# A long convolution on TensorE: sixteen chunks written out, or a loop of two chunks over fixed places

## What is computed

```python
dt = exp(log_dt); A = -exp(A_log)                       # 256 channels, 64 states
K = einsum('mn,mln->ml', C_re, exp(dt * A * t))         # one kernel of 512 taps for each channel
y = irfft(rfft(u, 2L) * rfft(K, 2L))[:L]                # causal convolution, channel by channel
x1 = x + y + u * D
```

## Time and profile before

| | |
|---|---|
| runs (us) | 989.84, 991.02, 986.16 |
| profiled execution, its own time (us) | 987.75 |
| its span, first to last instruction (us) | 985.9 |
| mean granted TensorE clock | 0.972 |
| busy share of the span | PE 93%, PEld 79%, ACT 53%, DVE 42%, POOL 29% |
| recurrence, about | 12 to 378.5 us of the span |
| convolution, first weight load of line 568 to the last addition's end | 388.3 to 463.0 us |
| chain that ended last | PE 85%, issue 5%, DVE 4%, ACT 4% |

### The profile page before, as it was taken

One profiled execution on the slowest core, in us unless ns is written; L12 is line 12 of the kernel. 1 busy time (PEld: TensorE's weight loads), 2 busy tenths in 40 slices (PEclk: granted clock), 3 DMA queues, 4 the chain that ended last, 5 costly groups with the idle time before them and its releaser, 6 DMA issues.

```text
span 985.9 us, 64681 instructions
## 1 busy us (share of the span) xinstructions
PE 919.4 (93%) x28784; PEld 774.4 (79%) x28784; DVE 411.2 (42%) x781; ACT 518.1 (53%) x1819; POOL 283.1 (29%) x310
## 2 busy tenths in 40 slices
PE   7999999999999998777999999999999999999993
PEld 5888888888888887666444445788899999999993
DVE  1000011000110004432698899875564655646450
ACT  2444444444444446662776776333465656656551
POOL 3111111111111111220001543762035455463545
PEclk6799999999999999998999999999999999999997
DMA  2222223221111110001000211343266666575634
GB/s 87 86 86 90 95 86 106 95 67 40 38 35 32 32 38 23 5 5 49 0 1 12 75 36 37 98 187 121 70 179 149 124 158 136 132 159 130 130 39 54
DMA packets 67163, 76.96 MB, mean 78 GB/s; under 512 B 24001, under 2 KB 53334, under 8 KB 67106
## 3 DMA queue, kind: packets, MB, share of 16 engines
q1 hardware_dynamic: 52226, 58.51, 19.1%
q0 software_dynamic: 14592, 17.10, 10.5%
q10 hardware_dynamic: 288, 0.56, 0.2%
HBM read 44.16 MB, written 33.83 MB: 79 GB/s over the span
## 4 chain that ended last, share of the span: by engine, by line
PE 85%; issue 5%; DVE 4%; ACT 4%; POOL 1%; DMA 0%; POOLq 0%; ACTq 0%; DVEq 0%
PE ps L503 19%; PE ps L789 17%; PE ps L495 8%; PE ps L803 8%; PE ps L655 8%; PE ps L705 6%; PE ps L476 6%; PE ps L732 3%; ACT tok L857 2%; PE ps L592 2%; PE ps L714 2%; PE ps L583 2%; PE ps L568 2%; PE ps L481 2%; POOL out L453 1%
## 5 line engine op out<-in xcount | busy, mean ns | idle before, releaser
L503 PE MATMUL ps<-tok,wh 128*32 128x8 f32 x16384 | 255.7, 180 | 12.9 <-issue 3.7
L857 ACT ACTIVATE tok<-ps 128x8 f32<-128x8 f32 x1024 | 156.3, 178 | 203.8 <-PE ps L503 199.5
L503 PEld LDWEIGHTS ps<-tok,wh 128*32 128x32 f32 x16384 | 220.4, 112 | 48.2 <-ACT tok L857 25.0
L453 POOL DMA_INDIRECT out<-arena,dest x80 | 127.9, 1599 | 99.2 <-ACT arena L1002 76.9
L476 PE MATMUL ps<-zero 128*32 128x192 bf16 x1920 | 141.4, 255 | 0.0
L789 PE MATMUL ps<-xgT_hi,ew_hi 128*128 128x320 f32 (+1 forms) x384 | 119.4, 311 | 2.9 <-DVE spare L1247 1.6
L407 POOL TENSOR_TENSOR big<-tok,zero 128x128 f32 x64 | 29.1, 455 | 322.0 <-ACT tok L857 322.0
L789 PE MATMUL ps<-xgT_hi,ew_lo 128*128 128x320 f32 (+1 forms) x384 | 119.6, 311 | 0.0
L789 PE MATMUL ps<-xgT_lo,ew_hi 128*128 128x320 f32 (+1 forms) x384 | 118.9, 310 | 0.0
L1115 DVE TENSOR_TENSOR arena<-arena,pack 128x256 f32 x32 | 13.6, 426 | 246.4 <-ACT arena L862 246.4
L1353 DVE TENSOR_TENSOR mid<-mid,ps 128x320 f32<-128x320 f32 (+1 forms) x96 | 46.7, 487 | 106.5 <-ACT mid L1020 64.4
(11 more groups left out here) (203 smaller groups left out, 1647.2 us busy)
## 6 DMA issues: line engine op xcount, KB each, us to landing
slots_in<-mid SPq DMA_DIRECT2D x16, 645.0 KB, 3.7
mid<-slots_in SPq DMA_DIRECT2D x16, 645.0 KB, 4.2
arena<-in_ex_down SPq DMA_DIRECT2D x16, 384.0 KB
arena<-in_ex_gate SPq DMA_DIRECT2D x16, 352.0 KB
arena<-in_ex_up SPq DMA_DIRECT2D x16, 352.0 KB
xst<-in_x_steps SPq DMA_DIRECT2D x66, 64.0 KB, 1.8
xtok<-in_x_tok SPq DMA_DIRECT2D x16, 256.0 KB, 2.7
mid<-k_pad SPq DMA_DIRECT2D x32, 128.0 KB, 3.1
```

Of the source, the lines that this page charges most:

```text
L453: pool.indirect_dma_start(out=out[:, :], out_offset=bass.IndirectOffsetOnAxis(ap=dest[:, z, t:t + 1], axis=0), in_=yo[:, z, t], in_offset= ...
L503: last = nc.tensor.matmul(sums_at(bank, t, o)[Q * j:Q * j + Q], wh[:, k, columns(j, o)], hring[:, (n - 1) % (2 * G), k], start=False, stop ...
L857: nc.scalar.activation(hring[:, n, o], sums_at(n // G, n % G, o), ACT.Tanh).then_inc(s_h[o], 1)
```

## The change

TensorE's chunks become a hardware loop of 8 passes, two chunks in each. A loop's body has fixed addresses, so `own_block(z)`, `block_states(z)` and `carried(z)` now read `tz`, `u_tok` and `qd` always at the places of chunks 0 and 1 (slot z). Later chunks are copied into these slots: `tz` by a DMA that SyncE issues once `own_block(m - 2)` is done (new semaphore `s_own`; `s_slot_tz` tells its landing), `u_tok` and `qd` by ScalarE (`steps_to_slot`, `decays_to_slot`, 128x512 each). The decays `d0` of all chunks are now made by GpSimd (one tensor_tensor of 128x512, as chunks 0 and 1 had before). TensorE's waits inside the loop are on register values, and ahead of each of the three groups stands one small matmul on zeros, `stand()`, of a 128x32 tile and 8 columns into bank 6. The order in a chunk becomes `own_block(m)`, `block_states(m + 1)`, `carried(m)`; the last pass makes one more `block_states`, which nobody reads.

```diff
@@ sync
-                sp.dma_start(tz[HB * k:HB * k + HB, P - CP:P], kt[k][:, P - CP:P]).then_inc(s_tz, 16)
+                sp.dma_start(tz[HB * k:HB * k + HB, P - CP:P], kt[k][:, P - CP:P]).then_inc(s_slot_tz[k], 16)
+            sp.wait_ge(s_tz, 16 * C * (NCH - 1))
+            for z in range(2):
+                sp.wait_ge(s_slot_tz[z], 16)
+            for m in range(2, NCH):
+                sp.wait_ge(s_own, m - 1)
+                sp.dma_start(tz[:, CP * (m % 2):CP * (m % 2) + CP], tz[:, CP * m:CP * m + CP]).then_inc(s_slot_tz[m % 2], 16)
@@ gpsimd, chunks 2 to 15
                 pool.wait_ge(s_tmm, m - 1)
                 power_args(m)
+                pool.wait_ge(s_xc, m)
+                block_decays(m)
@@ tensor
-            def own_block(m):
-                if m >= 2:
-                    pe.wait_ge(s_x1, m + 1)
+            def own_block(z):
                 for c in range(CP):
                     for k in range(C):
                         for odd in range(2):
-                            nc.tensor.matmul(to_tokens(m, c, k, odd), tz[rows_of_half(k), CP * m + c], ...
+                            last = nc.tensor.matmul(to_tokens(z, c, k, odd), tz[rows_of_half(k), CP * z + c], ...
+                last.then_inc(s_own, 1)
+            def stand():
+                nc.tensor.matmul(ps[0:Q, 6, 0:B], zero16[:, 0:Q], zero16[:, 0:B], start=True, stop=True, tile_position=(0, 0))
...
-            for m in range(NCH):
-                if m + 1 < NCH:
-                    block_states(m + 1)
-                own_block(m)
-                carried(m)
+            with pe.Fori(0, NCH // 2) as i:
+                for z in range(2):
+                    m = 2 * i + z
+                    pe.wait_ge(s_x1, m + 1)
+                    pe.wait_ge(s_slot_tz[z], 16 * i + 16)
+                    stand()
+                    own_block(z)
+                    pe.wait_ge(s_pe, m + 2)
+                    pe.wait_ge(s_xc, m + 1)
+                    pe.wait_ge(s_uea, 2 * m + SLOTS - 1)
+                    stand()
+                    block_states(1 - z)
+                    pe.wait_ge(s_xc, m + 2)
+                    pe.wait_ge(s_uea, 2 * m + SLOTS - 2)
+                    stand()
+                    carried(z)
@@ scalar
-            def block_decays(m):
-                act.wait_ge(s_xc, m - 1)
-                for c in range(CP):
-                    last = nc.scalar.activation(d0[:, m % 2, c], resets_t, ACT.Copy, scale=lam[:, CP * m + c:CP * m + c + 1])
-                last.then_inc(s_d0, 1)
+            def steps_to_slot(m):
+                act.wait_ge(s_own, m - 1)
+                to = CP * (m % 2)
+                nc.scalar.activation(u_tok[:, to:to + CP], u_tok[:, CP * m:CP * m + CP], ACT.Copy).then_inc(s_uea, 1)
+            def decays_to_slot(m):
+                act.wait_ge(s_qmm, m - 1)
+                to = CP * (m % 2)
+                nc.scalar.activation(qd[:, to:to + CP], qd[:, CP * m:CP * m + CP], ACT.Copy).then_inc(s_uea, 2 if m == NCH - 1 else 1)
...
             for m in range(2, NCH):
-                block_decays(m)
                 powers(m)
+                steps_to_slot(m)
+                decays_to_slot(m)
```

More of the change, by code:

```diff
@@ L231, in build @@
         s_late = sem("s_late")
+        s_own = sem("s_own")
+        s_slot_tz = [sem("s_slot_tz0"), sem("s_slot_tz1")]
         s_sum = [sem("s_sum0"), sem("s_sum1")]
@@ L247, in build @@
         NIN = 3 * (C + 1)
+        SLOTS = NB
         INPUTS = {1: (0, 1), 2: (1, 3), 3: (3, 4), 4: (4, 6), 5: (6, 7), 6: (7, NIN)}
@@ L557, in rows_of_half, with block_states @@
                 return slice(HB * k, HB * k + HB)
-            def block_states(m):
-                z = m % 2
-                pe.wait_ge(s_pe, m + 1)
-                if m >= 2:
-                    pe.wait_ge(s_xc, m - 1)
+            def block_states(z):
                 for c in range(CP):
@@ L567, in block_states, with to_tokens @@
                         to = ps[rows_of_half(k), z, RB * c:RB * c + RB].rearrange("p (b t) -> p b t", t=NB)[:, :, 1:NB]
-                        last = nc.tensor.matmul(to, pw[rows_of_half(k), z, c], u_tok[rows_of_half(k), CP * m + c].rearrange("p (b t) -> p b t", t=NB)[:, :, 0:NB - 1],
+                        last = nc.tensor.matmul(to, pw[rows_of_half(k), z, c], u_tok[rows_of_half(k), CP * z + c].rearrange("p (b t) -> p b t", t=NB)[:, :, 0:NB - 1],
                                                 start=True, stop=True, skip_group_check=True, tile_position=(HB * k, HB * k))
                 last.then_inc(s_tmm, 1)
-            def to_tokens(m, c, k, odd):
-                return ps[rows_of_half(odd), 2 + 2 * (m % 2) + k, 0:R * CP].rearrange("p (r c) -> p r c", c=CP)[:, :, c]
-            def own_block(m):
-                if m >= 2:
-                    pe.wait_ge(s_x1, m + 1)
+            def to_tokens(z, c, k, odd):
+                return ps[rows_of_half(odd), 2 + 2 * z + k, 0:R * CP].rearrange("p (r c) -> p r c", c=CP)[:, :, c]
+            def own_block(z):
                 for c in range(CP):
@@ L582, in own_block, with carried @@
                         for odd in range(2):
[L583 to L588, removed]
+                            last = nc.tensor.matmul(to_tokens(z, c, k, odd), tz[rows_of_half(k), CP * z + c], u_tok[rows_of_half(k), CP * z + c].rearrange("p (r e) -> p r e", e=2)[:, :, odd],
+                                                    start=c == 0, stop=False, skip_group_check=True, tile_position=(HB * k, HB * odd))
+                last.then_inc(s_own, 1)
+            def carried(z):
                 for c in range(CP):
@@ L591, in carried @@
                         for odd in range(2):
-                            last = nc.tensor.matmul(to_tokens(m, c, k, odd), qd[rows_of_half(k), CP * m + c], xc[rows_of_half(k), m % 2, c].rearrange("p (r e) -> p r e", e=2)[:, :, odd],
+                            last = nc.tensor.matmul(to_tokens(z, c, k, odd), qd[rows_of_half(k), CP * z + c], xc[rows_of_half(k), z, c].rearrange("p (r e) -> p r e", e=2)[:, :, odd],
                                                     start=False, stop=True, skip_group_check=True, tile_position=(HB * k, HB * odd))
                 last.then_inc(s_qmm, 1)
+            def stand():
+                nc.tensor.matmul(ps[0:Q, 6, 0:B], zero16[:, 0:Q], zero16[:, 0:B], start=True, stop=True, tile_position=(0, 0))
             pe.wait_ge(s_uev, NB)
-            pe.wait_ge(s_uea, NB)
-            pe.wait_ge(s_sz, 1)
+            pe.wait_ge(s_uea, SLOTS)
+            pe.wait_ge(s_xc, 1)
+            pe.wait_ge(s_pe, 1)
             block_states(0)
-            pe.wait_ge(s_tz, 16 * C * NCH)
+            pe.wait_ge(s_tz, 16 * C * (NCH - 1))
             pe.wait_ge(s_qd, IT)
-            for m in range(NCH):
-                if m + 1 < NCH:
-                    block_states(m + 1)
-                own_block(m)
-                carried(m)
+            with pe.Fori(0, NCH // 2) as i:
[14 more added lines that the diff above has]
+                    carried(z)
             def x1_turned(b):
@@ L869, in powers @@
                 act.wait_ge(s_pa, m + 1)
-                nc.scalar.activation(pw[:, m % 2], pw[:, m % 2], ACT.Exp, scale=consts[:, 4:5]).then_inc(s_pe, 1)
-            def block_decays(m):
-                act.wait_ge(s_xc, m - 1)
-                for c in range(CP):
-                    last = nc.scalar.activation(d0[:, m % 2, c], resets_t, ACT.Copy, scale=lam[:, CP * m + c:CP * m + c + 1])
-                last.then_inc(s_d0, 1)
+                nc.scalar.activation(pw[:, m % 2], pw[:, m % 2], ACT.Exp, scale=consts[:, 4:5]).then_inc(s_pe, 2 if m == NCH - 1 else 1)
+            def steps_to_slot(m):
[6 more added lines that the diff above has]
+                nc.scalar.activation(qd[:, to:to + CP], qd[:, CP * m:CP * m + CP], ACT.Copy).then_inc(s_uea, 2 if m == NCH - 1 else 1)
             powers(0)
@@ L880, in _ @@
             powers(1)
-            act.wait_ge(s_lam, 1)
+            act.wait_ge(s_uev, NB)
+            act.wait_ge(s_qd, IT)
             for m in range(2, NCH):
-                block_decays(m)
                 powers(m)
+                steps_to_slot(m)
+                decays_to_slot(m)
             act.preload_act_table(ACT.Sigmoid)
@@ L1130, in _ @@
                 dve.wait_ge(s_h[o], S + 1)
-            nc.vector.memset(ps[:, 0:2].rearrange("p n (c t) -> p (n c) t", t=NB)[:, :, 0], 0.0).then_inc(s_sz, 1)
+            nc.vector.memset(ps[:, 0:2].rearrange("p n (c t) -> p (n c) t", t=NB)[:, :, 0], 0.0).then_inc(s_xc, 1)
             u_out(dve, lambda to, v: nc.vector.tensor_copy(to, v), 0, s_uev)
```

5 lines of the change are left out of this document (3 added, 2 removed).

## The result

The changed kernel takes 975.0 us (median of 4 runs, 973.55 to 978.0) against 989.07 (4 runs of the kernel before on the same chip), a ratio of 0.9864, 95% interval 0.9829 to 0.99: faster by 1.4%. The prediction said 977.0, with a range of 965 to 985.

The account below looks back on a forecast made before the run. TensorE's convolution was taken as bound by its instruction fetch. Terms of 45.2 + 12.0 + 1.4 + 1.5 + 1.0 = 61.1 us of matmuls against 73.9 put the time at 977.0 us, range 965 to 985.

Parts of the forecast that it names:

- Fetch is the bound, and a loop removes it: TensorE's convolution waits some 1.5 us for each 16 KB instruction packet; q8 packets fall from 21 to about 4.
- Bodies of several packets are kept: The new loop body of 2.6 packets is not fetched again each pass, like the recurrence's 5.6 packets.
- rival 3: The convolution's loop fetches its body again in each pass: 17.7 us more, time 1,007; chance 6%.
- A chunk's base of 2.77 us and 0.25 us for each stand: Convolution: sixteen chunks at 2.77 us without fetches, plus 48 small matmuls with tile shape changes, 12.0 us in all.
- Rival 1: The convolution's small matmuls cost next to nothing, 1 us for all 48: time 966; chance 15%.
- Loop edges 0.2 us each: Each edge between passes of TensorE's loop costs 0.2 us, times 7 = 1.4 us.
- First pass 1.5 us, clock 1.0 us: Convolution loop: 1.5 us stall fetching the new body in the first pass, 1 us for a lowered TensorE clock.
- the first states: The 32 state matmuls ahead of the convolution's loop, put at 0.9 us.
- the 2.1 us added for the distance between profiled execution and median: Whole kernel: the profiled execution lay 2.1 us under the median, so 975.0 became a forecast of 977.0.
- Copies, decays and VectorE hidden: In the loop, other engines' work and the `tz` copy cost nothing, down to a chunk of about 2.9 us.
- Rival 2: Copies or register waits set the loop's pace, a chunk of 4.0 to 4.2 us: time 985; chance 10%.
- Rival 4: TensorE's clock stays at 1.2 GHz in the loop: 14.4 us more, time 1,004; chance 4%.

Follow-up runs that it names:

- e6: Changed kernel with its sixteen chunks written out instead of the hardware loop and no small matmul ahead of the groups: 996.68 us, ratio 1.0109.
- e4: Changed kernel with four chunks in a pass, four passes, small matmuls kept: 1012.84 us in one run.
- e7: Changed kernel with four chunks in a pass, register waits on nops and no small matmuls: 976.36 us, ratio 0.9883.
- e5: Changed kernel with eight chunks in a pass, two passes, small matmuls kept: 1013.52 us, ratio 1.0238.
- e2: Changed kernel with a nop carrying each register wait in place of the small matmul: 969.37 us, ratio 0.9787.
- e3: Changed kernel with each wait on a nop, followed by a small matmul of the groups' own 64x64 tile: 971.0 us, ratio 0.9849.
- e10: Changed kernel with one TensorE pause of 2.4 us between the first states and the loop: 1016.67 us, ratio 1.0278.
- e1: Changed kernel with only the hardware loop written out again, small matmuls kept: 1009.81 us, ratio 1.0193.
- e8: Kernel before, with only a small matmul of a 128x32 tile added ahead of each group: 1010.78 us, ratio 1.0221.

## Why the prediction was right

By its own steps:

- *Fetch is the bound, and a loop removes it*: shown. q8 21 to 4, "issue" ahead of the groups 19.1 us to 0.2, and with the loop written out again 21 packets are back and the convolution takes 75.9 us (e6).
- *Bodies of several packets are kept* (against rival 3): shown for 2.6 packets, and by e4 and e7 for 5.2. It ends before 10.3 (e5).
- *A chunk's base of 2.77 us and 0.25 us for each stand*: measured 3.53 a chunk, so (3.53 - 2.77) / 3 = 0.25 each and 12 us in all, as predicted. Its make-up was not as predicted, and that the total fits is in part luck. I put all of it down to two drains of 0.12 to 0.18 each and the register waits at nothing; e2 and e3 give the pair of shape changes 0.15 and leave 0.10 to the small matmul and the wait (which stays when the small matmul goes). Rival 1 was wrong for the changed kernel.
- *Loop edges 0.2 us each*: measured 0.20 in the changed kernel, 0.40 and 0.42 in e3 and e2, where a nop carries the wait.
- *First pass 1.5 us, clock 1.0 us*: measured 0.34 and 0. These two terms are 2.2 us too large. The sum is 1.5 too large (61.1 us of matmuls predicted, 59.6 measured, 60.4 less 0.8 for the last addition), since the first states took 1.1 us and not 0.9, and some 0.5 more lies in small amounts elsewhere. Of the 2.0 us between 977.0 and 975.0 the kernel has only 0.8: the profiled execution was put at 975.0 and took 974.19. The other 1.2 come from the 2.1 us added for the distance between profiled execution and median, which was 0.8 this time.
- *Copies, decays and VectorE hidden*: shown. At 3.53 us a chunk, and at 2.96 in e2, TensorE waits for none of them in the loop. Copies of 0.63 us and a `tz` copy of 2.3 us were within the bounds. Rival 2 was wrong.
- *Rival 4, the clock stays at 1.2 GHz*, had 4% and 1,004 us. For this kernel it did not come. The reason given against it (less idle time in all) was too weak: e10 differs from the changed kernel by one hole alone and fell, and the small matmuls which the change brought in turn a fall of some us into one for the whole loop. The cliff is 1016.7 us, deeper than I worked out, since a chunk there takes 5.97 us and not the 5.46 of the rival: the stands slow down as well (3.53 x 1.7 = 6.0). The longest hole in the changed loop is 0.34 us. With the same small matmuls e10 fell behind one of 2.38, and e1 behind three of 0.33, 0.84 and 0.91 within 9 us; what lies between was not tried. The prediction's time was right, the distance from this edge was not seen.

What remains open: why these small matmuls keep the clock down, and what exactly starts a fall. The length of the longest hole doesn't tell: e3 had holes of 0.94 and 1.81 us and stayed at 1.00, e2 fell behind one of 2.14, and e1 behind none over 0.91.

## What to carry to other kernels

Where the idle time of a busy engine is "issue" at an even pace and the instruction queue has the same pace, count instructions per packet: a loop whose body is kept (up to 5.6 packets here) is worth the small overheads it brings. Carry register waits on nops, not on small matmuls of another tile shape: here the nop version is 5.6 us faster than the changed kernel and keeps its time after a pause (972.9 us against 1,016.7). Look at the granted clock of every window before you explain a time; in five of the twelve experiments (e1, e4, e5, e8, e10) it stood at 0.50 for most of the convolution.

## What the hardware showed unexpectedly

- TensorE can be busy 6.00 of 6.00 us for 90 us (396 to 486) at a granted clock of 0.50 and not rise (e10), while its groups of 64x64 tiles are parted by small matmuls of a 128x32 tile. At 1.00 the same stream stays at 1.00 (the changed kernel).
- A body of 5.2 packets of 16 KB stays in reach of TensorE, one of 10.3 does not, and the jump back then costs 3.14 us.
- A pair of tile shape changes costs 0.15 us inside a chunk, a wait on a nop 0.06, a small matmul of the same tile 0.04, a loop's edge 0.20 with the 128x32 matmul behind it and 0.40 to 0.42 with a nop.
